# Leaving out table rows of slots without a node, and gathered rows of places without an edge, by indices beyond a bound

## The reference, cut to what matters

```python
k = typed_matmul(h, k_linears, node_type)          # per node, weights by node type
q = typed_matmul(h, q_linears, node_type)
v = typed_matmul(h, v_linears, node_type)
q_att = einsum('nhd,rhde->rnhe', q, relation_att)  # 8 relations, 4 heads of 64
v_msg = einsum('nhd,rhde->rnhe', v, relation_msg)
score = sum(q_att[etype, dst] * k[src], -1) * relation_pri[etype] / 8
alpha = softmax of score over the edges of one dst
agg   = segment_sum(alpha * v_msg[etype, src], dst)
out   = sigmoid(skip)[node_type] * typed_matmul(agg, a_linears, node_type)
```

## Time and profile before

| | us |
|---|---|
| timed, median of 3 runs (lowest, highest) | 2179.31 (2177.45, 2181.79) |
| span of the profiled execution | 2395.2 |
| of it TensorE busy | 1980.9 (83%) |
| VectorE busy | 1645.8 (69%) |
| ScalarE busy | 1468.0 (61%) |
| GpSimd busy | 1181.5 (49%) |

### The profile page before, as it was taken

How to read it: one execution, slowest core, us unless ns; L and a number is a source line. 1 busy time by engine, 2 the same in 40 slices (tenths; PEclk the granted TensorE clock), 3 DMA queues, 4 the chain that set the end, 5 groups by cost and what they waited for, 6 DMA issues and landing times.

```text
span 2395.2 us, 37397 instructions
## 1 busy us (share of the span) xinstructions
PE 1980.9 (83%) x10336; PEld 1471.8 (61%) x10336; DVE 1645.8 (69%) x3977; ACT 1468.0 (61%) x4981; POOL 1181.5 (49%) x1207
## 2 busy tenths in 40 slices
PE   6999997995788888888888888888888884753999
PEld 6865554554566766766666666666766663532666
DVE  8767764553677887787787877787787777585111
ACT  7755554562477677677677777677777675570221
POOL 0033334335466666566666666566665550621554
PEclk9999998997899999899999999899999997885999
DMA  7868878997688888788888988888888763682221
GB/s 253 283 234 323 323 302 266 335 389 246 219 257 259 270 267 260 253 271 261 268 264 252 289 254 264 253 260 267 271 262 258 253 215 108 190 286 63 75 76 46
DMA packets 271463, 583.72 MB, mean 244 GB/s; under 512 B 45079, under 2 KB 185963, under 8 KB 264601
## 3 DMA queue, kind: packets, MB, share of 16 engines
q0 software_dynamic: 93936, 384.51, 47.9%
q1 hardware_dynamic: 177320, 196.82, 25.9%
HBM read 407.81 MB, written 176.99 MB: 244 GB/s over the span
## 4 chain that ended last, share of the span: by engine, by line
PE 52%; DVE 18%; issue 11%; ACT 8%; another core or an unknown queue 7%; DVEq 2%; DMA 2%; POOL 0%; SPq 0%; POOLq 0%; ACTq 0%
PE bank L986 10%; PE bank L805 7%; PE bank L970 6%; ACT arena L1354 6%; PE bank L784 4%; PE bank L1144 4%; PE bank L1155 4%; DVE arena L1971 2%; PE bank L951 2%; DVE arena L2064 2%; PE bank L866 2%; PE bank L651 2%; PE bank L707 2%; PE bank L791 2%
## 5 line engine op out<-in xcount | busy, mean ns | idle before, releaser
L2377 POOL DMA_INDIRECT arena<-table,arena x880 | 866.7, 985 | 557.8 <-issue 215.2
L1354 ACT ACTIVATE arena<-arena 128x64 f32<-128x64 f32 x3448 | 841.4, 340 | 1.2 <-issue 1.1
L986 PE MATMUL bank<-arena 128*128 128x260 f32 x1760 | 479.4, 410 | 107.2 <-issue 68.9
L986 PEld LDWEIGHTS bank<-arena 128*128 128x128 f32 x1760 | 332.9, 200 | 213.2 <-issue 143.6
L1971 DVE TENSOR_TENSOR arena<-bank,arena 128x512 f32<-128x512 f32 x440 | 301.7, 687 | 191.4 <-remote 149.6
L970 PE MATMUL bank<-arena 128*128 128x256 bf16 x2640 | 345.6, 280 | 21.7 <-DVE arena L1971 11.2
L970 PEld LDWEIGHTS bank<-arena 128*128 128x128 bf16 x2640 | 265.1, 101 | 90.3 <-issue 16.2
L1981 DVE TENSOR_REDUCE arena<-arena 128x16 f32<-128x1024 f32 x220 | 267.8, 1217 | 17.2
L805 PE MATMUL bank<-arena 64*128 64x512 f32 x832 | 212.2, 625 | 24.0 <-DVE arena L1714 15.6
L2064 DVE TENSOR_TENSOR arena<-arena,bank 128x260 f32 x440 | 185.0, 421 | 64.4 <-remote 44.1
L1238 ACT COPY arena<-bank 128x512 f32<-128x512 f32 x260 | 148.9, 595 | 91.3 <-PE bank L805 81.1
(11 more groups left out here) (324 smaller groups left out, 3051.4 us busy)
## 6 DMA issues: line engine op xcount, KB each, us to landing
arena<-q_parts SPq DMA_DIRECT2D x440, 192.0 KB
arena<-chunk_rel SPq DMA_DIRECT2D x220, 128.0 KB
arena<-table,arena POOLq DMA_INDIRECT x880
node_rows<-arena SPq DMA_DIRECT2D x24, 512.0 KB, 6.4
xl_and_sum<-arena SPq DMA_DIRECT2D x3, 3072.0 KB, 17.5
arena<-in_x SPq DMA_DIRECT2D x12, 512.0 KB, 7.7
xn<-arena SPq DMA_DIRECT2D x12, 512.0 KB, 7.6
xT<-arena SPq DMA_DIRECT2D x12, 512.0 KB, 8.0
```

The source lines that it names most:

```text
L986: ins = TE.matmul(bank[b][:, 0:AW], lhsT=so[p % 2][:, c % 2, j, :], rhs=values_of(c, j), start=j == 0, stop=j == HALF - 1)
L1354: ins = A.activation(seg, seg, ACT.Copy, scale=rows[:, C + h:C + h + 1])
L2377: G.indirect_dma_start(rows_of_pair(p, i % 2 * HALF + j), None, d_tab_rows[0:N * R, :], bass.IndirectOffsetOnAxis(ap=idxE[:, g, j, c:c + 1 ...
```

## The change

The constant `NO_ROW` (2 to the power 20) is beyond any row of the table. The indirect DMAs of the slot stage's scatters and of the pass's gathers get a bound, above which an index's row is left out without an error (`oob_is_err=False`). For the scatters the bound is N - 1, so rows of slots without a node are not written. For the gathers it is the last row of the table, 8 N - 1, and `edge_marks` adds `NO_ROW` to the row of each place whose relative destination is 128 or more, but only in chunks from 36 on (`2 * RING_BLOCKS`), so that each block of the ring has been filled once. In what is not gathered the ring keeps older rows. Each bounded DMA is preceded on GpSimd by a register move for its bound. The output DMAs of the last stage (L2383) had such a bound before.

```diff
--- before.py
+++ after.py
@@ -89,6 +89,9 @@
 PAD_ROWS = N * R // (3 * P) - 1
 INV_PARTS = 4
 
+
+NO_ROW = 1 << 20
+
 COUNT_PARTS = 4
 
 CHOSEN = sum(len(rounds) for rounds in ROUNDS.values()) + 1
@@ -321,7 +324,7 @@
     start_i = tiny(CG, i32)
     offs = tiny(CG, i16).rearrange("p (o g) -> p o g", o=2)
     cmp_, pr = tiny(NT), tiny(NT)
-    ctile_p = tiny(CG)
+    ctile_p, skip_by = tiny(CG), tiny(CG)
     scale = [tiny(H) for _ in range(2)]
     f_arg = [tiny(H)[0:1, :] for _ in range(2)]
     top = tiny(H)[0:1, :]
@@ -1791,9 +1794,16 @@
             t = step(V.tensor_scalar(ctile_p, c_tile, float(P), None, ALU.mult))
             V.wait_ge(win_in, 16 * N_WIN)
             V.wait_ge(dve_step, t)
+            step(V.tensor_scalar(skip_by, iota_c, float(2 * RING_BLOCKS), float(NO_ROW), ALU.is_ge, ALU.mult))
             for g in range(CG):
                 t = step(V.tensor_scalar(drow[:, g, :], drow[:, g, :], ctile_p[:, g:g + 1], float(P), ALU.subtract, ALU.min))
             yield
+            V.wait_ge(dve_step, t)
+            for g in range(CG):
+                t = step(V.tensor_scalar(other[:, g, 0:CH], drow[:, g, 1:CH + 1], float(P), skip_by[:, g:g + 1], ALU.is_ge, ALU.mult))
+            yield
+            V.wait_ge(dve_step, t)
+            t = step(V.tensor_tensor(out=irow[:, :, 1:CH + 1], in0=irow[:, :, 1:CH + 1], in1=other[:, :, 0:CH], op=ALU.add))
             V.wait_ge(dve_step, t)
             V.tensor_copy(rel_bf, drow[:, :, 1:CH + 1]).then_inc(rel_ready, 1)
             yield
@@ -2343,13 +2353,15 @@
                 gather_x(s + NGX)
             if s + 1 < NTS:
                 G.wait_ge(q_low, s + 2)
-                G.indirect_dma_start(d_q3[:, :], at_nodes(node_i, s + 1), q3[(s + 1) % NKQV].rearrange("p s n -> p (s n)"), None).then_inc(q_out.sem(s + 1), 16)
+                G.indirect_dma_start(d_q3[:, :], at_nodes(node_i, s + 1), q3[(s + 1) % NKQV].rearrange("p s n -> p (s n)"), None,
+                                     bounds_check=N - 1, oob_is_err=False).then_inc(q_out.sem(s + 1), 16)
             if s >= 0:
                 for m in range(4):
                     for h2 in range(2):
                         b, k = psum.at("tab", s, m, h2)
                         G.wait_ge(empty[b], k)
-                G.indirect_dma_start(d_tab[:, :], at_nodes(node_i, s), tabs[s % NTAB].rearrange("p r n -> p (r n)"), None).then_inc(tab_out.sem(s), 16)
+                G.indirect_dma_start(d_tab[:, :], at_nodes(node_i, s), tabs[s % NTAB].rearrange("p r n -> p (r n)"), None,
+                                     bounds_check=N - 1, oob_is_err=False).then_inc(tab_out.sem(s), 16)
             if s == WINDOW_SLOT:
                 place_edges()
 
@@ -2375,7 +2387,8 @@
                 g, c = divmod(i, P)
                 for j in range(HALF):
                     G.indirect_dma_start(rows_of_pair(p, i % 2 * HALF + j), None, d_tab_rows[0:N * R, :],
-                                         bass.IndirectOffsetOnAxis(ap=idxE[:, g, j, c:c + 1], axis=0)).then_inc(rows_in.sem(p), 16)
+                                         bass.IndirectOffsetOnAxis(ap=idxE[:, g, j, c:c + 1], axis=0),
+                                         bounds_check=N * R - 1, oob_is_err=False).then_inc(rows_in.sem(p), 16)
 
 
         def put_out(s):
```

## The result

The changed kernel takes **2191.76 us** (median of 6 runs, 2188.66 to 2202.07); the kernel before, measured beside it, 2180.31 (6 runs). The ratio is 1.0053, 95% interval 1.0036 to 1.0069: 11.6 us slower, between 8 and 15. I had forecast 2165 and given 0.11 to slower. The rows ahead of the prediction come from an execution with a span of 2395.2 us. Which chip it ran on is not on record; it looks like the executions of one chip, of the five that the experiments used, on which the kernel before takes 2387 us. On the other four it takes 2183 to 2185.

What follows compares the result with a forecast made beforehand. The pass was taken as a loop of waits, with 97 us of late transfers. 6.1 + 6.4 + 8.6 - 4 - 1 = 16.1 us of the profiled 2395.2, scaled to 14.7, gave 2165 us; range 2138 to 2186.

Steps and rivals of the forecast that it cites:

- What bounds the kernel now: Pass as a loop of waits, 6.4 us a pair; unnamed releaser at L1971 taken for late gathers, 97 us of chain.
- Middle pairs: Pairs 28 to 208 of the pass: 6.5% fewer gathered rows shrink 97 us of lateness by 6.4 us; bounds 0 and 55.
- pairs 209 to 219: Last pairs of the pass gather nothing, so VectorE's waits of 9.2 us there give 8.6 us; bounds 0 and 16.6.
- hidden anyway: Rival: profiling lengthens the stops for transfers, so little is left of the gains; time 2175 to 2182, chance 0.19.
- Start of the pass: Empty scatters of slots 50 and 51 let the first gather start 7.0 us sooner; `expand` next late; gain 6.1 us.
- Price of the bounded gather: GpSimd's gathers in the pass: 34 ns more each, judged by bounded scatters, landing later at VectorE's 59 stops; cost 4 us.
- a bounded gather costs more: Rival: each extra d us per gather in the pass delays landings by 236 d; 2203 at d = 0.2, chance 0.11.
- half way to the bounds: Sum in the rival that transfers set the pace more widely: 7 + 27 + 12, less 5, 41 us; 2142, chance 0.12.
- VectorE's six instructions: Added in the slot stage, 2.5 us in two slots, partly covered by 2.42 us idle; cost 1 us, bounds 0 and 2.5.
- Left-out rows still cost their issue: GpSimd's indirect DMAs: all 984 instructions stay and nothing is issued less often, though rows are not moved.

Runs made afterwards that it cites:

- e0_before: The kernel before, unchanged, profiled a second time on one of the other four chips: ratio 1.0 [0.9981, 1.0018], profiled span 2187.5 us.
- e8_late_again: The kernel before with bounds only on the scatters of slots 31 to 51, gathers unbounded: ratio 0.9977 [0.9968, 0.9987], -5.0 us.
- e2_bound_only: The kernel before with the bound on the gathers alone, no index beyond it, scatters as before: ratio 1.0057 [1.0037, 1.0078], +12.4 us.
- e4_moves: The kernel before with unused register moves meant ahead of slot scatters, absent from the program; slower chip: ratio 0.9991, median 2383.5 beside 2387.1.

## Why the prediction was wrong, step by step

**"What bounds the kernel now"** is where it failed first. It read 195 pairs of 6.4 us, 1.5 us of slack a pair for GpSimd, and 97 us of late transfers on the path. In `e0_before` a pair takes 5.6 us (180 pairs from the 28th on, 1007 us), GpSimd's slack is 0.5 us, and the unnamed releaser is absent. I had noticed that the profiled execution was 216 us longer than the timed ones and scaled the sum by 0.91. What was called for was to ask which stage holds the excess. From the first gather to the last it is 1414.7 us in the first profile and 1225.9 in `e0_before`: 189 of the 208 us between the two spans lie in the pass. The gains of the middle and the end, 15 of the 21 us, were taken from waits that belong to this excess.

**Middle pairs, 6.4 us, and pairs 209 to 219, 8.6 us.** Both terms are parts of the missing 97 and 9.2 us. Measured together: about 2 us, not told from zero. In the last eleven pairs the gathers land 2.4 us after their issue and not 4.4 (medians from 1712 to 1768 us, changed kernel and `e0_before`), and nothing comes of it. The rival "hidden anyway" was right that these gains would not show and wrong on the reason, that profiling lengthens the stops: `e0_before` was profiled too, and its span is 2187.5.

**Start of the pass, 6.1 us.** The mechanism was right, with 5.8 us by profile (4.2 in place of 10.0) against 7.0 for the gather. Pair 0's first product starts 19.2 us after scatter 51 in `e0_before` and 14.5 in `e8_late_again`, 4.7 us sooner against the 6.1 of the sum. What is late next is not `expand` on TensorE, as forecast, which ends at 539.4 us in `e8_late_again`, but VectorE's own work before the product, which ends at 540.7 after a wait of 6.54 us for ScalarE (L1305). The gain reaches the end: -5.0 and -6.3 us in the two kernels without the idle stretch at the jump. The sum lacked what the scatters' moves do to the code behind them: +7.4 us measured by itself. No rival had it.

**Price of the bounded gather, -4 us.** This term was undersized by 8 us, and it was wrong twice. First, 52 ns and not 34: a bounded scatter was the wrong yardstick for a bounded gather. The changed kernel's own table scatters take 983 ns in the median and its gathers 998; without a bound they take 956 and 946. Second, and larger, how much reaches the end. The route was right, rows that land later where VectorE waits for them, but I let each of 59 stops grow by one pair's delay and put 1.5 us of slack before it. GpSimd issues 671 of 758 gathers with nothing but the gap of an issue before them, so the delay adds up from gather to gather until its next wait for TensorE, and the stops themselves become more, 8 to 20. 880 x 0.052 = 46 us less the slack that it can still use leave 12.4. The rival "a bounded gather costs more" had this route and slower as its outcome, but its formula 236 d gives 12.3 us at d = 0.052, with which its own sum is still a gain, 21.1 - 12.3 - 1 = 8 us. That 12.3 is near 12.4 is chance: its 59 stops don't exist here.

Two slips of the working change nothing of this. From a pair of 6.4 us GpSimd sets the pace at d = 0.35 and not 0.36. And "half way to the bounds" is 6.6 + 30.7 + 12.6 less 5, 45 us and not 41.

**VectorE's six instructions, -1 us:** nothing measured, within bounds. **Left-out rows still cost their issue:** right, "nothing is issued less often"; the gathers of the last eleven pairs, whose places are all empty, take 998 ns in the median like all others. The Trainium skill (DMA: Bandwidth & Descriptors, "SWDGE vs HWDGE vs iDMA") says that a core of GpSimd computes the bytes of the descriptors in software. The traces show packets and not descriptors; that the packets of q0 stay 93936 fits it.

**The sum, as measured:** 12.4 to 13.5 for the bound, -2 for the rows, -6 for the start, +7 for the place of the code: 11 to 13 us, each term with an interval of a few us; the changed kernel 11.6.

## What to carry to other kernels

Before pricing a gain, compare the profiled span with the timed runs: if they differ by more than the effect, find the stage that holds the difference, and build no term on it. An indirect DMA with a bound is dearer for every instruction, and the rows that it drops saved bytes and no issue time here; put it where transfers are waited for (here: the last scatters before a stage that waits for them), and leave it off where the issuing engine is near the pace. A null result of a dummy load counts only once the trace shows that the load moved something, and after adding instructions look for new idle time with no releaser at jumps. Take a pace from what an engine needs per turn of the loop and from its waits, and not from its share of one chain.

## What was not expected of the hardware

- **A jump over unused code can hold an engine for 9 to 12 us.** GpSimd's idle time at the same jump is 0.65 to 0.68 us in the kernels with the code in its old place or 128 instructions on, and 9.40, 11.07 and 12.26 us with 63 more; the last of these kernels, without any bound, is 7.4 us slower. The instruction queues show blocks being loaded. `e0_before` and `e2_bound_only`, whose difference is 880 moves on GpSimd:

```profile
q14 instruction: 120, 0.98, 0.1%
```

```profile
q14 instruction: 127, 1.04, 0.1%
```

- **A bound costs a gather of 128 rows 52 ns on GpSimd** (946 to 998), whether it is an immediate or a register (1002) and whether rows are beyond it or not; with every second gather bounded it is 949 and 1011. A table scatter goes from 956 to 983.
- **One write, or three, of 128x1 between two indirect DMAs of GpSimd add 0 to 0.02 us**, since they fit the 0.30 us that stand there; a wait for the write's end makes it 0.08.
- **One chip of five takes 9% longer.** The kernel before takes 2183 to 2185 us on four and 2387 on the fifth. The last table scatter is issued at most 12 us later there (541.69 in e4_moves, 529.77 in `e0_before`), and the difference arises in the pass, where the DMA engines' share from 640 to 1700 us is 0.84 and not 0.91. TensorE's mean granted clock is 0.935 and not 0.951. The cause is open. The bound in a register (10 us) and the late scatters (-6) come out much as elsewhere, but the gathers with rows left out cost 23 us [15, 32] in place of 11 [8.5, 14].
